# Wide attentions: building the folded key and value products with VectorE summing the constant row and ScalarE copying both halves of VW

## The reference

```python
kh = jnp.concatenate([kh, jnp.broadcast_to(bias_k, (b, 1, H, K))], axis=1)
vh = jnp.concatenate([vh, jnp.broadcast_to(bias_v, (b, 1, H, K))], axis=1)
logits = jnp.einsum('bqhk,bthk->bhqt', qh, kh) / scale
weights = jax.nn.softmax(logits, axis=-1)
ctx = jnp.einsum('bhqt,bthk->bqhk', weights, vh).reshape(b, q_len, H * K)
return ctx @ wo + bo
```

## Time and profile before

| what | value |
|---|---|
| median of three runs | 957.06 us (953.86 to 961.48) |
| profiled execution, time (its span; no other is given) | 957.6 us |
| TensorE busy | 881.7 us (92%) |
| VectorE busy | 604.0 us (63%) |
| ScalarE busy | 491.8 us (51%) |
| GpSimd busy | 484.3 us (51%) |

### The profile page before, as it was taken

The page is one execution under the profiler, slowest core; times in us unless marked ns, Lnnn a source line. Parts: engine busy times, 40 slices in busy tenths (PEclk is TensorE's granted clock), DMA queues, the critical chain, the costliest instruction groups (busy, mean ns, idle before and its releaser), DMA issues.

```text
span 957.6 us, 15739 instructions
## 1 busy us (share of the span) xinstructions
PE 881.7 (92%) x5624; PEld 737.2 (77%) x5624; DVE 604.0 (63%) x1344; ACT 491.8 (51%) x1205; POOL 484.3 (51%) x507
## 2 busy tenths in 40 slices
PE   4889876899999999999899898899999999999898
PEld 3677755899966789666797787899975689757788
DVE  3688887416779757796423545325779867798440
ACT  2566655654753356533663332764763347632662
POOL 2667876474543345465293170184544335465383
PEclk8699999999999999999999988999999999999999
DMA  6823312002550025200002000101570015200001
GB/s 188 294 91 87 102 38 96 5 2 72 168 213 1 1 70 162 100 1 0 23 2 88 1 2 0 64 37 40 160 254 0 1 35 164 67 1 1 1 12 34
DMA packets 26673, 64.04 MB, mean 67 GB/s; under 512 B 2995, under 2 KB 15843, under 8 KB 25444
## 3 DMA queue, kind: packets, MB, share of 16 engines
q1 hardware_dynamic: 26596, 63.03, 20.2%
HBM read 57.22 MB, written 5.77 MB: 66 GB/s over the span
## 4 chain that ended last, share of the span: by engine, by line
PE 70%; DVE 19%; issue 5%; POOL 3%; ACT 1%; DMA 1%; SPq 1%; DVEq 0%; POOLq 0%
PE ps L964 7%; PE ps L904 6%; PE ps L863 6%; PE ps L865 6%; PE ps L893 5%; PE ps L940 4%; PE ps L762 3%; PE ps L705 3%; PE ps L706 3%; PE ps L707 3%; PE ps L686 3%; DVE prob L1658 3%; PE ps L687 3%; PE ps L688 3%; DVE mx L1657 3%
## 5 line engine op out<-in xcount | busy, mean ns | idle before, releaser
L964 PE MATMUL ps<-arena,pT_all 128*128 128x256 f32 x512 | 116.6, 381 | 5.7 <-DVE x L1678 3.6
L964 PEld LDWEIGHTS ps<-arena,pT_all 128*128 128x128 f32 x512 | 96.2, 190 | 32.3 <-issue 15.1
L940 PE MATMUL ps<-arena,hT 128*128 128x512 f32 x256 | 115.5, 594 | 0.0
L536 POOL TENSOR_TENSOR rstd<-var,neg_half 128x1 f32<-128x1 f32 (+1 forms) x56 | 33.9, 606 | 155.1 <-DVE var L1487 155.1
L543 POOL TENSOR_TENSOR arena<-arena,rinv 128x640 f32<-128x640 f32 x64 | 80.4, 1257 | 55.4 <-DVE rinv L1472 55.3
L570 POOL TENSOR_TENSOR prob<-prob,rinv 128x512 f32<-128x512 f32 x32 | 49.5, 1547 | 113.2 <-DVE rinv L1671 113.2
L1196 ACT ACTIVATE arena<-ps,nb 128x320 f32<-128x320 f32 x128 | 66.4, 523 | 58.1 <-DVE nb L1458 57.9
L1239 ACT ACTIVATE arena_r<-ps,cols 128x256 fp32r<-128x256 f32 x128 | 66.5, 520 | 55.1 <-PE ps L688 55.0
L512 POOL TENSOR_TENSOR vacc<-vacc,vpart 128x256 f32<-128x256 f32 x60 | 44.0, 734 | 98.6 <-ACT vpart L1311 98.3
L589 POOL TENSOR_TENSOR arena_r<-arena,arena_r 128x512 fp32r<-128x512 f32 x64 | 83.9, 1333 | 13.2 <-ACT arena L1240 13.2
L686 PE MATMUL ps<-hH,w1H 128*128 128x256 f32 x256 | 75.2, 294 | 11.9 <-DVE prob L1658 5.1
(11 more groups left out here) (164 smaller groups left out, 2350.9 us busy)
## 6 DMA issues: line engine op xcount, KB each, us to landing
ring<-in_heads_dram SPq DMA_DIRECT2D x64, 512.5 KB, 3.6
w<-in_w_dram SPq DMA_DIRECT2D x8, 1024.0 KB, 7.3
first_r<-spare_k SPq DMA_DIRECT2D x24, 160.0 KB
first_q<-spare_q SPq DMA_DIRECT2D x48, 64.0 KB, 2.6
spare_k<-HL SPq DMA_DIRECT2D x8, 320.0 KB, 2.4
spare_q<-HL SPq DMA_DIRECT2D x8, 256.0 KB, 2.3
x<-in_x_dram SPq DMA_DIRECT2D x1, 1024.0 KB, 6.0
lnb<-in_lnb_dram SPq DMA_DIRECT2D x4, 256.0 KB, 6.6
```

The lines of the kernel that those rows point to most:

```text
L940: last = mm(ps[:, SCORES[k][half], :], hT[:, k, d, 0:P], A[:, d, b // 2, cols_of, sl, :].rearrange("p r s k -> p r (s k)"), start=(d == 0) ...
L964: last = mm(ps[:, 6, 0:D], pT[:, k, c, :], VW[:, b, c, :], start=(c == 0), stop=(c == PAIRS - 1))
```

## The change

VectorE takes over the constant row: behind `wq` of each head, one pass scales the head's output weights by `bias_v` and adds them to `vacc` (for head 0 it only scales). `vpart` and its semaphore are gone from ScalarE and GpSimd; the room of the tile stays reserved. ScalarE copies both halves of `VW`, and VectorE's copy and the semaphore `vw_dve` are gone. SyncE's ring loads wait for `vacc_ready` where they waited for `vpart_ready`, here and in front of the load of `wp2`; the waits for `vw_dve` go from TensorE's products and from the scores of the second tile. The diff, cut to its core, in the order SyncE, GpSimd, TensorE, ScalarE, VectorE (twice):

```diff
@@ -397,7 +395,7 @@
                         sp.wait_ge(vw_ps, n - RING + 1)
-                        sp.wait_ge(vpart_ready, n - RING + 1)
+                        sp.wait_ge(vacc_ready, n - RING + 1)
...
@@ -501,15 +499,6 @@
...
-                    pool.wait_ge(vpart_ready, n + 1)
-                    if h == 0:
-                        if a > 0:
-                            pool.wait_ge(crow_ps, a)
-                        g.tensor_copy(vacc[:, :], vpart[:, k, :]).then_inc(vacc_ready, 1)
-                    else:
-                        pool.wait_ge(vacc_ready, n)
-                        g.tensor_tensor(vacc[:, :], vacc[:, :], vpart[:, k, :], ALU.add).then_inc(vacc_ready, 1)
@@ -899,7 +888,6 @@
...
                         pe.wait_ge(vw_act, n - 1)
-                        pe.wait_ge(vw_dve, n - 1)
...
@@ -1306,10 +1293,6 @@
...
-                        if n >= 2:
-                            act.wait_ge(vacc_ready, n - 1)
-                        a_(vpart[:, k, :], ring[:, n % RING, WO:WO + D], ACT.Copy, scale=col(f"{l}_bias_v{i}", step))\
-                            .then_inc(vpart_ready, 1)
...
                         act.wait_ge(vw_ps, n + 1)

+                        a_(VW[0:C, h % 2:B:2, h // 2, :], ps[0:C, 4 + k, :].rearrange("p (g n) -> p g n", g=2), ACT.Copy)
                         a_(VW[C:P, 1 - h % 2:B:2, h // 2, :], ps[C:P, 4 + k, :].rearrange("p (g n) -> p g n", g=2),
                            ACT.Copy).then_inc(vw_act, 1)
@@ -1556,6 +1540,15 @@
...
+                wo, bias_v = ring[:, n % RING, WO:WO + D], col(f"{l}_bias_v{i}", h)
+                if h == 0:
+                    if a > 0:
+                        dve.wait_ge(crow_ps, a)
+                    v.tensor_scalar(vacc[:, :], wo, bias_v, None, ALU.mult).then_inc(vacc_ready, 1)
+                else:
+                    dve.wait_ge(vacc_ready, n)
+                    v.scalar_tensor_tensor(vacc[:, :], wo, bias_v, vacc[:, :], ALU.mult, ALU.add)\
+                        .then_inc(vacc_ready, 1)
@@ -1614,16 +1607,9 @@
...
-                for h in range(H):
-                    n = a * H + h
-                    k, par = n % 2, h % 2
-                    if h + 1 < H:
-                        weights(a, h + 1)
-                        keys_rest(a, h + 1)
-                    dve.wait_ge(vw_ps, n + 1)
-
-                    v.tensor_copy(VW[0:C, par:B:2, h // 2, :], ps[0:C, 4 + k, :].rearrange("p (g n) -> p g n", g=2))\
-                        .then_inc(vw_dve, 1)
+                for h in range(1, H):
+                    weights(a, h)
+                    keys_rest(a, h)
```

More of the change, by code:

```diff
@@ L160, in build @@
         u = sb("u", [P, 2, D])
-        vpart = sb("vpart", [P, 2, D])
+        vpart_room = sb("vpart_room", [P, 2, D])
         KC = arena[:, 9728:13824].rearrange("p (m b n) -> p m b n", m=4, b=B)
@@ L274, in build @@
         wq_ready = sem("wq_ready")
-        vpart_ready = sem("vpart_ready")
         vacc_ready = sem("vacc_ready")
@@ L282, in build @@
         vw_act = sem("vw_act")
-        vw_dve = sem("vw_dve")
         z_ready = sem("z_ready")
@@ L452, in _ @@
             sp.wait_ge(vw_ps, 2 * H)
-            sp.wait_ge(vpart_ready, 2 * H)
+            sp.wait_ge(vacc_ready, 2 * H)
             sp.dma_start(wp2, t["wp2"]).then_inc(in_l2, 16)
@@ L932, in scores @@
                         pe.wait_ge(vw_act, H * (a + 1))
-                        pe.wait_ge(vw_dve, H * (a + 1))
                     elif g >= 2:
```

## The result

| | before | after |
|---|---|---|
| median of the first measurement, 20 runs each | 956.15 us | 959.21 us |
| ratio, 95% interval | | 1.0037 [1.0019, 1.0055] |
| ratio of a second measurement (12 runs beside 35) | | 1.0016 [0.9992, 1.0039] |
| profiled execution: its time (its span) | span 957.6 | 959.44 (957.2) |

One run of 2265.06 us (before, first measurement) and one of 4985.85 us (after, second measurement) were disturbed and are left out of the ratios.

A forecast was written before the change was run, and what follows sets the result against it. TensorE, gapless in the buildings, was taken as the bound. Inside 0 + starts 0 + ends 1.5 us, put on the three-run median 957.06, gave 958.6 us, called no change (under 1%); range 953 to 964.

The forecast's parts named there:

- inside the building: Middle heads: ScalarE, VectorE and GpSimd changes stay hidden under TensorE's 3.31 us a head; cost 0.
- the starts: Start of a building: first vacc write delays the first K remainder 0.48 to 0.83 us, still hidden by 0.15 at worst; cost 0.
- the ends: Last head: two VW halves at 0.61 a step delay head 15's A copy and the scores by 0.37; four ends, 1.5 us.
- 0.5 us a head was to be left idle: ScalarE in middle heads: two half copies at 0.61 each fit in 1.73 us, leaving 0.5 us idle.
- rival 5: Inside buildings, ScalarE becomes the pace from 0.86 us a half; at 1.0 a half +17 us, 974; chance 0.04.
- 1.0 was given: VectorE in middle heads: slack of 1.0 us before the K remainder, which waits for the next V.
- Rival 2: VectorE late for the last K remainder, vacc pass and u colliding: 0.8 us on top of the forecast, 959.4; chance 0.09.
- Rival 4: Buildings paced by VectorE, its relief of 0.41 a head showing in 60 heads: 25 us faster, 932; chance 0.03.
- Rival 1: At building ends, ScalarE's halves overlap, 0.50 a step: only +0.6 us, 957.7; chance 0.17.
- Rival 3: Before a building's last products, the K remainder comes earlier and removes TensorE's 0.28 us idle: -1.1 us, 957.5; chance 0.07.
- 13 us less busy: VectorE's total busy time: expected to fall some 13 us, 64 x 0.20, as a sign that the forecast is right.

The follow-up runs named there:

- e1: Changed kernel with the lower-half VW copy back on VectorE, constant row staying there: 956.90 us, ratio to before 1.0005 [0.9986, 1.0025]; buildings 49.34 to 49.35 us.
- e3: Changed kernel with head 15's A copy moved ahead of head 14's upper VW half on ScalarE: 955.80 us, ratio to before 0.9989; buildings 49.34 us.
- e6: Changed kernel plus one unneeded copy of head 14's upper VW half before head 15's A copy: 961.14 us, ratio to before 1.0062 [1.0030, 1.0094].
- e4: Changed kernel with head 15's K remainder ahead of its values and its A copy ahead of both head 14 VW halves: 957.04 us, ratio to before 1.0017.
- e5: Changed kernel with only head 15's K remainder put ahead of its values: 958.27 us, ratio to before 1.0034 [1.0007, 1.0062]; buildings 49.70 to 49.71 us.
- e2: Changed kernel with the constant row back on ScalarE and GpSimd, both VW halves staying on ScalarE: 959.04 us, ratio to before 1.0028 [1.0006, 1.0049].

## Why the prediction was right

**The forecast.** No change was right, and so was its cause. It gave 0 inside the building, 0 at the starts and 4 x 0.37 at the ends; the buildings are longer by 0.37, 0.36, 0.39 and 0.36, 1.5 in all. e1 and e3 show that nothing else of the change is in them. The first timed difference is 3.1 us; the second, 958.61 - 956.33 = 2.3, is nearer. Neither excess was found in a stretch of the trace. That the time itself came out so close, 958.6 forecast and 959.21 measured, is luck: the median that it started from, 957.06, was 0.9 above that of the 20 runs (956.15), and the timed difference was larger than the sum by 1.6.

**Inside a building.** One middle head of after, ScalarE and VectorE, as the earlier trace rows:

```profile
258.11 0.48 DVE L1557 SCALAR_TENSOR_TENSOR HL<-ps,kvd,HL 128x256 fp32r<-128x256 f32 x1 [0.80 <-ACT VT L1295]
...
258.82 0.59 ACT L1305 ACTIVATE arena<-ps 64x512 f32<-64x512 f32 x1 [0.26 <-PE ps L892]
...
259.42 0.59 ACT L1306 ACTIVATE arena<-ps 64x512 f32<-64x512 f32 x1
260.10 0.47 DVE L1550 SCALAR_TENSOR_TENSOR vacc<-ring,cols,vacc 128x256 f32<-128x256 f32 x1
260.55 0.47 ACT L1292 ACTIVATE HL<-ps,kvd 128x256 fp32r<-128x256 f32 x1 [0.53 <-PE ps L854]
```

On ScalarE 0.5 us a head was to be left idle; ahead of the K copy (L1292) the trace has 0.53. A lower half takes 0.59, mean 590 ns over 64, as the upper one: rival 5 (ScalarE sets the pace) has nothing left. On VectorE the pass (L1550) mostly takes 0.47 to 0.48 as forecast (mean 502 ns; 0.93 at 253.16, beside `u`). In 56 of 64 heads VectorE waits for V before the K remainder, by 0.44 to 1.19 us and 46.7/56 = 0.83 on average, where 1.0 was given; in the others, the first two of each building, no weight load waited for it. Rival 2 needed that slack gone at the ends, where it is 1.17 to 1.18. Rival 4 (VectorE as the pace) needed a head shorter than 3.30; 42.94/13 is 3.30.

**Starts.** The first remainder was to stay hidden by 0.15 us at worst. The start of the first building in after, as the earlier trace rows:

```profile
219.49 0.48 DVE L1541 SCALAR_TENSOR_TENSOR wq<-u,rho,wq 128x256 fp32r<-128x256 f32 x1
...
219.89 0.35 DVE L1547 TENSOR_SCALAR vacc<-ring,cols 128x256 f32<-128x256 f32 x1
...
221.54 0.47 DVE L1557 SCALAR_TENSOR_TENSOR HL<-ps,kvd,HL 128x256 fp32r<-128x256 f32 x1
...
223.17 0.87 PE L882 MATMUL ps<-HL,wq 128*128 128x256 f32 x6
```

The remainder ends at 221.54 + 0.47 = 222.01 and its products go at 223.17: 1.16, more than the 0.98 of before (224.14 to 225.12). The `vacc` write costs 0.35, and the `wq` pass ahead of it takes 0.48 where it took 0.83.

**Ends.** From the lower half of head 14 to the A copy of head 15 the trace has 273.24 - 272.02 = 1.22, the forecast's 2 x 0.61. Rival 1 (0.50 a step) falls by it. But the ground for 0.61 was in part luck: the prediction took the missing overlap from copies of half height, and two copies of half height do overlap in e6 (0.50 a step); the last section has what the pairs that do not overlap have in common. Rival 3 falls too: the wait for the K remainder is 0.28 as before. But the price put on that wait, up to 1.1 us, was too high: with it gone and nothing else late (e4) it is 4 x 0.14.

**What failed, without a cost in time.** VectorE was to be 13 us less busy (64 x 0.20); the page has 604.0 and 601.5. The step took 0.68 out and 0.48 in and left its other operations as they were. Groups by line, before and after:

```profile
L503 POOL TENSOR_TENSOR u<-ring,lnb 128x256 f32<-128x256 f32 x64 | 67.7, 1057 | 0.0
...
L1625 DVE COPY arena<-ps 64x512 f32<-64x512 f32 x64 | 43.7, 682 | 16.2 <-PE ps L904 16.2
...
L1557 DVE SCALAR_TENSOR_TENSOR wq<-u,rho,wq 128x256 fp32r<-128x256 f32 x64 | 31.7, 495 | 2.3
...
L1556 DVE TENSOR_SCALAR wq<-u,rho 128x256 fp32r<-128x256 f32 x64 | 22.6, 354 | 33.5 <-DVE rho L1551 33.1
```

```profile
L501 POOL TENSOR_TENSOR u<-ring,lnb 128x256 f32<-128x256 f32 x64 | 46.1, 723 | 137.9 <-DMA ring<-in_heads_dram 122.7 <-DVE wq L1541 15.1
...
L1541 DVE SCALAR_TENSOR_TENSOR wq<-u,rho,wq 128x256 fp32r<-128x256 f32 x64 | 35.0, 546 | 2.3
L1540 DVE TENSOR_SCALAR wq<-u,rho 128x256 fp32r<-128x256 f32 x64 | 33.8, 527 | 2.3
...
L1550 DVE SCALAR_TENSOR_TENSOR vacc<-ring,cols,vacc 128x256 f32<-128x256 f32 x60 | 30.1, 502 | 0.0
L1547 DVE TENSOR_SCALAR vacc<-ring,cols 128x256 f32<-128x256 f32 x4 | 1.4, 348 | 0.0
```

VectorE's copy goes (-43.7), the constant row comes (30.1 + 1.4), and the two `wq` lines grow by 11.2 + 3.3: these lines come to +2.3. (The lines add up records, and neighbouring records overlap: the pass at 219.89 begins before `wq` ends at 219.97. So they do not add up to the page's -2.5.) At the same time GpSimd's `u` shrinks from 1057 to 723 ns. `u` now starts when its DMA has landed, no longer behind a `vacc` addition, and so beside `wq` instead of beside the sum `rho`. That this shifts the cost from the one to the other is read from the rows; no run changed that order alone. e1, where VectorE has its copy again, fits: `u` stays at 770 ns and the `wq` lines are at 382 and 488, but `rho` takes 576 where before has 424 and after 444.

## What to carry to other kernels

Where one engine is gapless, as TensorE is in these buildings, moving work between the others was free until the place where its list runs out: there, count what stands in front of the one copy that releases the next phase, and move whatever nobody waits for behind it. A wait removed at such a place is worth nothing while a second one ends later (e5), and less than its idle time when it goes (0.14 for 0.28), since here the loads ran ahead of the matmuls. An effect of 0.15% is read from the lengths between marks around the edited place, here a building, which agree to 0.02 us within a trace, rather than from times that scatter by 2.7.

## What the runs showed of the hardware

**Neighbouring copies on ScalarE overlap only sometimes.** With copies of 0.59 us, the next one started after 0.47 to 0.51 where both begin at the same partition (A copy to lower half in after, e2, e4 and e5; upper to upper in e6) and after 0.59 to 0.62 where the first partition changes between 0 and 64 (lower to upper, A to upper, upper to A, upper to lower). The pair of 0.26 and 0.27 in the earlier trace rows, which the prediction leaned on for its half height, goes from partition 0 to 64 as well; e6 shows that half height is not the cause. That it is the partition where the copy starts fits every pair seen here, but no run varied it alone. The Trainium skill, "ScalarE: Activation LUTs", section "What ACT_TABLE_LOAD costs", says that back-to-back activations overlap by about 93 ns: the first kind of pair agrees (0.59 - 0.50 = 0.09), the second does not.

**Where VectorE and GpSimd meet, which of them takes longer changed with the program.** One head of after, VectorE and GpSimd:

```profile
259.04 0.86 POOL L501 TENSOR_TENSOR u<-ring,lnb 128x256 f32<-128x256 f32 x1 [2.41 <-DMA ring<-in_heads_dram]
259.35 0.83 DVE L1541 SCALAR_TENSOR_TENSOR wq<-u,rho,wq 128x256 fp32r<-128x256 f32 x1
```

Here `u` began first, and `wq` took 0.83; at 269.27, where no `u` ran, it took 0.48. In the kernel before, what ran beside `u` (261.17, 1.20) was not `wq` but the sum `rho`:

```profile
261.37 0.41 DVE L1551 CUSTOM_DVE_ANT_0 sq<-ring,lnb 128x257 f32<-128x257 f32 x1
```

By the records `u` began first there too, by 0.20 us, but `rho` kept its 0.41 and `u` was the longer one (its shortest in that trace is 0.63). The Trainium skill, "SBUF — State Buffer", section "Who interferes with whom", says that a VectorE instruction with two inputs in SBUF contends with a GpSimd instruction that reads SBUF, and that "Issue order, not op shape, decides who blocks." That the two meet at a cost agrees. That the order decides is not shown: the later one paid in after and the earlier one in before, by the starts that the profile records.
